# Source chunks in a new order: the attention of an LSTM decoder step on TensorE

## The reference, cut to what matters

```python
def attend(h):
    q = h @ Wq.T
    scores = jnp.einsum('bc,bsc->bs', q, context)
    alpha = jax.nn.softmax(scores, axis=-1)
    ctx = jnp.einsum('bs,bsc->bc', alpha, context)
    return jnp.tanh(jnp.concatenate([ctx, h], axis=-1) @ Wout.T + b_out)

def step(carry, x_t):
    h, c, attn = carry
    inp = jnp.concatenate([x_t, attn], axis=-1)
    gates = inp @ W_ih.T + b_ih + h @ W_hh.T + b_hh
    i, f, g, o = jnp.split(gates, 4, axis=-1)
    c = jax.nn.sigmoid(f) * c + jax.nn.sigmoid(i) * jnp.tanh(g)
    h = jax.nn.sigmoid(o) * jnp.tanh(c)
    attn = attend(h)
    return ((h, c, attn), attn)

_, outs = jax.lax.scan(step, init, xs)      # 512 steps
```

## Time and profile before

| | |
|---|---|
| median of 3 runs | 6507.48 us (6506.85 to 6508.93) |
| profiled execution | 6506.8 us, its span 6504.8 us |
| PE busy in the span | 5746.6 us (88%) |
| DVE busy in the span | 3742.4 us (58%) |
| ACT busy in the span | 2001.6 us (31%) |

### The profile page before, as it was taken

The page is one execution under the profiler, slowest core; times in us unless marked ns, Lnnn a source line. Parts: engine busy times, 40 slices in busy tenths (PEclk is TensorE's granted clock), DMA queues, the critical chain, the costliest instruction groups (busy, mean ns, idle before and its releaser), DMA issues. The chain is left out here.

```text
span 6504.8 us, 332594 instructions
## 1 busy us (share of the span) xinstructions
PE 5746.6 (88%) x145488; PEld 3981.4 (61%) x145488; DVE 3742.4 (58%) x16358; ACT 2001.6 (31%) x7480; POOL 290.9 (4%) x779
## 2 busy tenths in 40 slices
PE   6899999999999999999999999999888779795979
PEld 2577777777777777777777777777444334443433
DVE  4355555555555555555555555554387998888852
ACT  3133333333333333333333333333122222222221
POOL 0000000000000000000000000000011011111000
PEclk8999999999999999999999999999998889897989
DMA  1100000000000000000000000000211101010111
GB/s 65 53 2 2 2 2 2 2 2 2 2 2 2 2 2 2 2 2 2 2 2 2 2 2 2 2 2 9 68 39 33 34 24 48 24 55 17 42 32 55
DMA packets 42841, 105.28 MB, mean 16 GB/s; under 512 B 7912, under 2 KB 9960, under 8 KB 42240
## 3 DMA queue, kind: packets, MB, share of 16 engines
q1 hardware_dynamic: 41312, 103.13, 5.1%
q10 hardware_dynamic: 1440, 1.06, 0.1%
HBM read 93.64 MB, written 10.52 MB: 16 GB/s over the span
## 5 line engine op out<-in xcount | busy, mean ns | idle before, releaser
L650 PE MATMUL lstm_part_ps<-lstm_keys,lstm_hid 128*4 128x128 f32 x32768 | 989.0, 273 | 206.2 <-DVE lstm_hid L795 206.2
L650 PEld LDWEIGHTS lstm_part_ps<-lstm_keys,lstm_hid 128*4 128x4 f32 x32768 | 823.0, 87 | 341.4 <-DVE lstm_hid L795 324.6
L666 PE MATMUL lstm_ctx_ps<-lstm_values,lstm_alpha 128*4 128x128 f32 x32768 | 988.2, 273 | 0.0
L666 PEld LDWEIGHTS lstm_ctx_ps<-lstm_values,lstm_alpha 128*4 128x4 f32 x32768 | 820.9, 87 | 79.9
L608 PE MATMUL lstm_half_ps<-lstm_w_hid,lstm_hid 128*13 128x96 f32 x16384 | 690.1, 247 | 0.0
L822 DVE TENSOR_REDUCE lstm_neg_max<-lstm_part_ps 128x1 f32<-128x128 f32 x1024 | 298.5, 292 | 519.0 <-PE lstm_part_ps L650 444.9
L762 ACT ACTIVATE lstm_expo<-lstm_part_ps,lstm_neg_max 128x128 f32<-128x128 f32 x1024 | 376.5, 368 | 713.9 <-DVE lstm_neg_max L822 713.9
L780 DVE STREAM_TRANSPOSE lstm_gates<-lstm_half_ps 128x96 f32<-128x96 f32 x1024 | 289.8, 283 | 441.1 <-PE lstm_half_ps L608 417.2
L847 DVE TENSOR_SCALAR lstm_out_row<-lstm_ctx_ps,lstm_factor 128x128 f32<-128x128 f32 x512 | 179.4, 350 | 580.2 <-PE lstm_ctx_ps L666 580.2
L608 PE MATMUL lstm_half_ps<-lstm_w_attn,lstm_attn 128*13 128x96 f32 x16416 | 501.5, 247 | 1.4 <-ACT lstm_attn L773 0.7
L769 ACT ACTIVATE lstm_out_row<-lstm_ctx_ps,lstm_factor 128x128 f32<-128x128 f32 x512 | 188.9, 369 | 736.4 <-PE lstm_ctx_ps L666 736.4
(11 more groups left out here) (331 smaller groups left out, 8371.6 us busy)
## 6 DMA issues: line engine op xcount, KB each, us to landing
mix_ring<-in_sm_chunks SPq DMA_DIRECT2D x120, 358.0 KB, 2.9
mix_ring<-in_mix_chunks SPq DMA_DIRECT2D x64, 384.0 KB, 3.0
lstm_xg<-xg_rows SPq DMA_DIRECT2D x514, 16.0 KB
xg_rows<-lstm_xg_tile SPq DMA_DIRECT2D x16, 512.0 KB, 2.6
ctxT<-in_ctxT SPq DMA_DIRECT2D x1, 2048.0 KB, 15.1
out_xT<-xT SPq DMA_DIRECT2D x4, 512.0 KB, 3.8
xT<-in_xT SPq DMA_DIRECT2D x1, 1536.0 KB, 10.1
lstm_w_x<-in_lstm_w_x SPq DMA_DIRECT2D x1, 1024.0 KB, 8.7
```

The costliest lines, as they stand in the source:

```text
L650: mm = pe.matmul(part_rows(score_ps[part], b), hid[:, k, lo:lo + SPACE], keys[:, k, b * SRC + c * P:b * SRC + (c + 1) * P], start=(n == 0 ...
L666: mm = pe.matmul(part_rows(ctx_ps[o], b), alpha[:, b, c, SPACE - 1 - c:2 * SPACE - 1 - c], values[:, b * SC + c, o * P:(o + 1) * P], start ...
```

## The change

TensorE takes the source chunks in another order. `scores` now takes one chunk `c` in place of a part. After the first hidden chunk come the scores of chunks 0, 1 and 2; the wait for the second hidden chunk then stands ahead of the rest, and chunks 0 and 1 (part 0) are finished before chunk 3 is begun. `turn(0)` stands ahead of both `half_hid(0, .)`, and these ahead of the contexts. The contexts of chunk 0 begin on the first `alpha_ready`; `turn(1)` stands between the contexts of chunk 0 and those of chunk 1. On VectorE, `keep_turned(t, 0)` goes ahead of the transpose of the two maxima. The number of matmuls is the same.

```diff
-                def scores(part, k):
-
-                    for n in range(2):
-                        c = 2 * part + n
-                        for b in range(BATCH):
-                            lo = PAD + SPACE * b - c
-                            mm = pe.matmul(part_rows(score_ps[part], b), hid[:, k, lo:lo + SPACE],
-                                           keys[:, k, b * SRC + c * P:b * SRC + (c + 1) * P],
-                                           start=(n == 0 and k == 0), stop=(n == 1 and k == KC - 1))
+                def scores(c, k):
+
+                    part, n = c // 2, c % 2
+                    for b in range(BATCH):
+                        lo = PAD + SPACE * b - c
+                        mm = pe.matmul(part_rows(score_ps[part], b), hid[:, k, lo:lo + SPACE],
+                                       keys[:, k, b * SRC + c * P:b * SRC + (c + 1) * P],
+                                       start=(n == 0 and k == 0), stop=(n == 1 and k == KC - 1))
                     return mm
@@
                         pe.wait_ge(h_ready[0], t + 1)
-                        for part in range(PARTS):
-                            scores(part, 0)
+                        for c in (0, 1, 2):
+                            scores(c, 0)
                         pe.wait_ge(h_ready[1], t + 1)
-                        for part in range(PARTS):
-                            scores(part, 1).then_inc(scores_ready, 1)
+                        scores(0, 1)
+                        scores(1, 1).then_inc(scores_ready, 1)
+                        scores(3, 0)
+                        scores(2, 1)
+                        scores(3, 1).then_inc(scores_ready, 1)
                         hidden_part()
-                        half_hid(0, 0)
                         pe.wait_ge(exp_ready, 2 * t + 1)
                         turn(0)
+                        half_hid(0, 0)
                         half_hid(0, 1)
+                        pe.wait_ge(alpha_ready, 2 * t + 1)
+                        for o in range(KC):
+                            context(0, o)
                         pe.wait_ge(exp_ready, 2 * t + 2)
                         turn(1)
-                        pe.wait_ge(alpha_ready, 2 * t + 1)
-                        for c in (0, 1):
-                            for o in range(KC):
-                                context(c, o)
+                        for o in range(KC):
+                            context(1, o)
                         pe.wait_ge(alpha_ready, 2 * t + 2)
@@
+                        keep_turned(t, 0)
                         dve.wait_ge(max_ready, 2 * t + 2)
                         dve.transpose(spread_blocks(spread_max[:, :]), every_row(neg_max[:, :])).then_inc(max_spread, 1)
-                        keep_turned(t, 0)
                         dve.wait_ge(max_spread, t + 1)
```

## The result

The changed kernel takes 6534.85 us in the median of 6 runs (6530.45 to 6535.97), the kernel before 6507.41 us (6 runs, 6505.92 to 6508.93): a ratio of 1.0041, 95% interval 1.0032 to 1.0051. It is slower by 27 us, 0.4%.

The account below looks back on a forecast made before the run. The prediction took the loop's once-a-step chain, up to the contexts' end on PE, as the bound. Insertion 0.37 less earlier start 0.335 gave +0.035 us a step, 18 us over 512 steps: 6525.5 us, range 6503 to 6538.

Parts of the forecast that it names:

- Scores, order: Score matmuls: a 0.09 hole opens at the second hidden chunk; part 0 whole 0.12 earlier, part 1 0.10 later.
- the hole of 0.09: In the scores ahead of the fourth block: PE waits for the second hidden chunk, needed at +0.66, seen at +0.75.
- First exponential, both half_hid behind turn(0), contexts of chunk 0: Step's middle: turn(0) from +2.40 to +2.28, half_hid from +2.53, contexts from +2.87, 0.335 us earlier.
- turn(1) between contexts: Second transpose, between context blocks: pays a 0.11 drain, starts at +3.42, next context 0.26 later; 0.37 us inserted.
- the sign of being wrong: Load of turn(1) starting less than 0.15 behind the last context matmul's start would make the prediction wrong.
- Contexts of chunks 2 and 3: Later contexts: second copy seen at +4.01, needed at +4.12; factor at +4.55, needed about +4.81; nothing paid.
- Sum: Whole step: insertion 0.37 less earlier start 0.335, +0.035 us a step, 18 us over 512 steps; 6525.5 us.
- the forecast case itself: Whole kernel: the step 0.035 us longer, 6525.5 us, own range 6518 to 6534; chance 0.66.
- PE's own work up to the contexts' end: PE in a step of the kernel before: 4.3 us in blocks, plus two transposes, the rest holes.
- the faster ones: At turn(1)'s load: no drain between contexts; insertion 0.26 gives 6469 us, lower bound 0.12 gives 6397 us; chance 0.08.
- The late hand-over: Second copy over 0.10 late, or first exponential not earlier: up to 0.155 a step, 6587 us; slower than 6535: chance 0.09.
- the slack of 0.10: Before chunk 2's contexts: the margin between the second copy being seen and chunk 2 needing it.

Follow-up runs that it names:

- b_scores_only: Against the changed kernel: scores kept in the new order, the rest of TensorE's order as before the change; 6507.14 us, ratio 1.0000 to the kernel before.
- d_turn_again: Changed kernel plus one more transpose a step, between the contexts of chunks 1 and 2, into columns nobody reads; 6718.67 us, ratio 1.0325.
- c_strips: Changed kernel with each turn as four 32-column strip matmuls against the whole identity in place of one transpose; 6539.2 us, ratio 1.0049.
- a_tail_only: Changed kernel with the scores back in the old order, the rest of TensorE's and VectorE's order as changed; 6591.83 us, ratio 1.013.
- g_eight_new: Changed kernel with each turn as four strip matmuls streaming only the eight identity columns the copy wants; 6371.47 us, ratio 0.9791.

## Why the prediction was right

By its own steps:

- *Scores, order.* Right: the hole of 0.09, part 0 whole about 0.12 earlier (its reduce starts at +1.43, before +1.56), part 1 0.10 later (+1.84 for +1.85). The hole costs nothing by itself behind the old tail: b_scores_only stands at 1.0000.
- *First exponential, both half_hid behind turn(0), contexts of chunk 0.* Right to 0.01: +2.27, +2.53, +2.87.
- *turn(1) between contexts.* Right: 0.37 in the timeline (0.12 and 0.25 in d_turn_again), 0.359 a step by that run's time. The load starts 0.20 behind the last context matmul's start, where less than 0.15 was named as the sign of being wrong. The drain comes with the change of tiling mode (the width of the weights): with strips alone in the loop the load side has no hole there, and at L1472 it comes without a transpose. The rule of the Trainium skill's "TensorEngine Tiling (Array Packing)", Key Properties, that a change of mode drains TensorE, agrees with the traces of the changed kernel and of c_strips. The Trainium skill's "TensorE: Matmul & The Clock Gate", Part 2, has weight loads pulled ahead of matmuls in flight; that agrees with the strips (no idle ahead of the turn's loads) and not with the transpose (0.22 idle), so here it is seen only within a mode.
- *Contexts of chunks 2 and 3.* Right: neither the copy (over at 2005.23 + 0.17 = 2005.40, +3.95; six blocks take 1.31, as without a wait) nor `factor` (written at 2006.00, used at 2006.25) held anything.
- *Sum.* The mechanism was right and its size too small: 0.035 a step forecast, 0.042 in the trace, 0.038 on steps without a branch and 0.046 on those with one. 18 us became 21.6 in the loop, 2.2 lie outside it, and the timed runs are 27 us longer. In the loop the term that was mis-sized is the step with a branch, which I priced like the others: 0.011 too little on 256 steps, 2.8 of the 3.6 us. That is not the whole of it: in a_tail_only (0.164 a step for 0.155) the steps without a branch carry the excess (8.447 against 8.280 us, 0.166), for there contexts begin at +3.00 and not at +2.99. What the remaining 4 us of the timed runs are, no trace shows. Steps with a branch vary between 8.45 and 8.61 us in the trace of the changed kernel, enough to hold them, but that is a guess. The median of 6534.85 lies 3 us inside the range of 6503 to 6538 and 1 us outside the 6518 to 6534 that I gave the forecast case itself, so the size came out right only roughly.
- *PE's own work up to the contexts' end.* Misread, without effect on the sum: not 4.3 us but 1.75 + 0.21 + 2 x 0.16 + 1.75 = 4.0.

The rivals: the faster ones fell with d_turn_again (0.26 or 0.12 an insertion would be 133 or 61 us). The late hand-over did not occur in the changed kernel; it did in c_strips and g_eight_new, where the insertion was shorter or the copy later, and the slack of 0.10 was used up.

## What to carry to other kernels

A matmul of another tiling shape inside a stream of strips cost more than its own time here; look where it stands before moving it, because the same transpose was partly hidden in a wait before and paid in full after. Ask also how much of it is needed: eight columns in place of 128, and on strips, were worth 134 us, five times what the order had cost. And when a rewrite removes one cost and the total stands still, read the timeline before dropping the theory: in c_strips the drain was gone and the way to the copy was longer.

## What the runs showed of the hardware that was not expected

- A loop body of four steps in place of two costs 951 us (7458.42 against 6507.45): the instruction queue moves 23.69 MB in place of 0.74, TensorE's loads wait twice for 3.3 us on average behind each of the branches, and behind the first wait the granted clock is at about half (0.54 over 6.6 us). At two steps the branch costs 0.18 us and the clock stays full. Where between the two bodies it turns was not tried.
- A change between 128 and 64 columns of weights put 0.09 to 0.10 between two plain matmuls at L1472, in either direction; in the loop, from strips to 128 columns, it was 0.11.
- A consumer sees a block of eight strip matmuls with 128 columns 0.50 us behind its start, a single transpose of the same data 0.37 behind it.
- The granted clock stayed at full (2.4 GHz) in the loop of the changed kernel, as in the earlier trace rows, so the difference between the two orders does not come from it.
